# A decoder layer on one core: the order of the attention turns and of the start

## The chip, the cores and the metric

The kernel runs on one core of a Trainium2 chip. The metric is the device time of one execution in microseconds; lower is better. A core has five engines that run side by side, each in its own order: TensorE (PE, matrix products and transposes into PSUM banks), VectorE (DVE), ScalarE (ACT), GpSimd (POOL) and SyncE (SP, which here only issues DMAs). They wait for each other by semaphores.

## What is computed

One pre-norm decoder layer on x (32 sequences of 128 tokens, width 512), a context of 32 x 128 x 256 and two positions for each token:

```python
x = x + attn(layernorm(x))               # 16 heads of 32, rotary, causal
x = x + cross_attn(layernorm(x), ctx, pos)  # 32 heads of 16, axial rotary, + bout
x = x + ffn(layernorm(x))                # silu(gate) * up, 1408 wide, int weights with scales
```

Self-attention has q, k, v and output products with 512 x 512 weights. Cross-attention takes q from x and k, v from the context (one weight Wkv, 256 x 1024). Each softmax runs over the 128 keys of a sequence.

## The kernel before, in words

All products of the attention part are made of three passes with split operands: high half by high half, high by low, low by high, summed in one PSUM bank (`project`, L446). So each weight and each transposed activation needs a high half, made by ScalarE (a copy to the rounded type), and a low half, made by VectorE or GpSimd (original less high half).

The attention part is a software pipeline over the 32 sequences. `schedule` (L300) calls, on every engine, the function `turn(sq, cq, nx, nz, oq)`. In one turn five sequences are in work: `nz` is loaded and normalised, `nx` gets its self-attention q, k, v products, `sq` its self-attention scores, softmax and output product, `cq` its cross-attention (two rounds of 16 heads, called 2a and 2b), `oq` its last products with v and the output product. Turns 0 to 3 are written out, 27 turns run in a loop (`TURNS`), and four more follow. What each engine does in a turn, and in which order, is fixed by the order of the lines in its `turn`.

PE's turn before (L519): scores 1 (a mask product and 32 small products); the spread reciprocals of `oq` transposed (bank TC), `attend2("2b")` of `oq` (L501, products of the transposed probabilities with v); Wq2 product; Wo2 product; the v half of Wkv; T(q2); `transpose_prob("1")`; reciprocals of `sq` transposed; scores 2a; `attend1`; Wq1 product of `nx`; the k half of Wkv of `sq` (k2, TC); Wo1 product; `transpose_prob("2a")`; T(q1); scores 2b; `attend2("2a")`; Wk1 and Wv1 products; T(k2); `transpose_prob("2b")`; T(k1); T(z1), T(z2). Here T(k1) is the transpose of the rotated keys, and `collect` (L488) makes PE wait for the copies of transposed probabilities out of PSUM.

A rotated q or k is made in three steps: `rope` on VectorE (L778), two operations of 128 x 512 out of PSUM, then `rope_sum` on GpSimd (L380), one addition of two SBUF tiles, then the transpose on PE. q1 and q2 share one scratch buffer, k1 and k2 another. `spread` (L384) on GpSimd widens the reciprocals of the row sums to the head width; PE transposes them into TC, ScalarE copies them to rT1 or rT2 (L682, L669), and VectorE multiplies (`normalise_ctx`, L822). `normalise` (L766) is VectorE's layer norm: three operations on one element a partition, then z (L775), 128 x 512 from SBUF to SBUF. In a loop turn VectorE also reduces a window of the feed-forward weights (L915).

ScalarE's turn before (L661): rT2, the exponentials of scores 1 (L652, four banks of four), v2 and q2 copies, odd copies, rT1, exponentials and odd copies of 2a, q1 copy, exponentials 2b, v1 copy, odd copies 2b, high halves of z1T and z2T. VectorE copies the transposed k1 (L930).

At the start SyncE loads x of sequence 0, positions, then seven weights of 1 MB each. VectorE first makes the rotary angles (L730 to L754), then the norm of sequence 0, then the low halves of the first three weights; ScalarE makes the sines, the high halves of all seven weights in order, and loads the table for the exponentials (L709).

The lines around the last scores in PE's turn:

```python
                if has_c:
                    collect("2a", cq)
                    scores2("2b")
                    ...
                    attend2("2a")
                if has_n:
                    ...  # Wk1 and Wv1 products
                if has_s:
                    pe.wait_ge(rot["k2"], sq + 1)
                    transpose4(TC, columns(RA["k2"])).then_inc(rT_d["k2"], 1)
                if has_c:
                    transpose_prob("2b", cq)
                if has_n:
                    pe.wait_ge(rot["k1"], nx + 1)
                    transpose4(PA, columns(RA["k1"])).then_inc(rT_d["k1"], 1)
```

## Time and profile before

| | us |
|---|---|
| median of 3 runs | 1823.09 (1822.44 to 1823.45) |
| the profiled execution | 1822.44 |
| its span, first to last instruction | 1820.7 |
| PE matmul busy | 1693.9 (93%) |
| PE weight loads busy | 1376.9 (76%) |
| VectorE busy | 1158.4 (64%) |
| ScalarE busy | 964.3 (53%) |
| GpSimd busy | 480.6 (26%) |
| DMA, mean | 44 GB/s |

PE carries the work; the other engines set at which moments it has to wait. A share over the whole span says little here, as the start, the loop, the last turns and the feed-forward part (from about 1306 us) have different limits. In the rows of a timeline the first number is the start in us from the span's start, the second the time from the first start to the last end of the merged instructions, then engine, line, operation, what is written and read, shapes, and in brackets the idle time of the engine before it with what ended it.

### The profile page before, as it was taken

Reading aid. Unit: us, or ns where it says so; the run is one execution under the profiler, and the core shown is the slowest. Engines: PE = TensorE matmul, PEld = TensorE weight load, DVE = VectorE, ACT = ScalarE, POOL = GpSimd, SP = SyncE. Lnnn points to the kernel's source line nnn. Section 1 sums busy time; section 2 is a strip of 40 time slices with the busy share of each in tenths; the row PEclk is TensorE's granted clock in tenths of the full one; section 3 lists DMA queues with packets and bytes.
Section 4 is the critical chain, followed back from the end, with each engine's and each line's share of the span. In section 5 each row is a group of like instructions: output and inputs, shape, how many; then the busy total and the mean of one; then the engine's idle time right before and its main releaser. Section 6 shows DMA issues by size and latency. Waiting matters only on the chain. (4 is left out here: it accounts for less than half of the span.)

```text
span 1820.7 us, 36475 instructions
## 1 busy us (share of the span) xinstructions
PE 1693.9 (93%) x12704; PEld 1376.9 (76%) x12736; DVE 1158.4 (64%) x2143; ACT 964.3 (53%) x3791; POOL 480.6 (26%) x470
## 2 busy tenths in 40 slices
PE   4799999999999999999999999997899999999997
PEld 2577777777777777777777777776688888888885
DVE  4677777777777777777777777765564343444432
ACT  4366666666666666666666666665542222222221
POOL 1233333333334333343333333333001110110111
PEclk8899999999999999999999999998799999999999
DMA  5010110000101001010010100101332101110110
GB/s 194 15 32 19 32 46 28 33 28 28 50 28 33 28 28 50 28 33 28 28 50 28 33 28 28 36 29 58 107 107 70 69 0 69 69 59 10 69 46 24
DMA packets 55094, 80.93 MB, mean 44 GB/s; under 512 B 4880, under 2 KB 25488, under 8 KB 55056
## 3 DMA queue, kind: packets, MB, share of 16 engines
q1 hardware_dynamic: 55056, 80.43, 13.6%
q8 instruction: 24, 0.39, 0.1%
q14 instruction: 14, 0.11, 0.0%
HBM read 63.63 MB, written 16.78 MB: 44 GB/s over the span
## 5 line engine op out<-in xcount | busy, mean ns | idle before, releaser
L652 ACT ACTIVATE prob<-bank,nmax 128x128 f32<-128x128 f32 x1536 | 537.3, 405 | 108.3 <-DVE nmax L833 108.3
L652 ACT ACTIVATION_READ_ACCUMULATOR prob<-bank,nmax 128x1 f32 x1536 | 377.5, 246 | 0.0
L833 DVE TENSOR_REDUCE nmax<-bank 128x4 f32<-128x512 f32 x384 | 241.2, 684 | 97.0 <-PE bank L478 70.9
L1109 PE MATMUL fbank<-shared,piece_hi 128*128 128x512 f32 x1152 | 280.3, 394 | 0.0
L1109 PEld LDWEIGHTS fbank<-shared,piece_hi 128*128 128x128 f32 x1152 | 215.8, 187 | 53.2
L382 POOL TENSOR_TENSOR rope_buf<-rope_buf 128x512 f32<-128x512 f32 x128 | 165.2, 1291 | 300.3 <-DVE rope_buf L790 300.0
L456 PE MATMUL bank<-shared,z1T_h 128*128 128x512 f32 x768 | 204.3, 409 | 5.1 <-DVE shared L947 3.8
L443 PE MATMUL bank<-ident,prob 128*128 128x128 f32 x1536 | 191.9, 278 | 10.9 <-ACT prob L652 10.9
L1261 DVE SCALAR_TENSOR_TENSOR h<-fbank,su_c,sil 128x512 f32<-128x512 f32 x88 | 66.0, 750 | 206.1 <-PE fbank L1109 199.0
L443 PEld LDWEIGHTS bank<-ident,prob 128*128 128x128 f32 x1536 | 174.8, 143 | 20.5 <-ACT prob L652 16.5
L659 ACT ACTIVATE probT<-bank 128x512 f32<-128x512 f32 x192 | 115.3, 600 | 130.9 <-PE bank L443 130.8
L456 PEld LDWEIGHTS bank<-shared,z1T_h 128*128 128x128 f32 x768 | 142.0, 191 | 47.3 <-issue 16.4
L1195 ACT ACTIVATE sil<-fbank,sg_c 128x512 f32<-128x512 f32 x88 | 60.4, 687 | 174.6 <-PE fbank L1109 172.2
L1201 ACT ACTIVATE h_h<-h 128x512 fp32r<-128x512 f32 x88 | 55.6, 632 | 175.8 <-DVE h L1261 175.8
L839 DVE COPY probT<-bank 128x512 f32<-128x512 f32 x192 | 126.5, 685 | 17.0 <-PE bank L443 13.0
L401 POOL TENSOR_TENSOR cn_l<-cn,cn_h 128x512 fp32r<-128x512 f32 x64 | 82.7, 1292 | 186.0 <-DVE cn L825 186.0
L388 POOL TENSOR_TENSOR rbc<-rinv,one_c 128x512 f32<-128x512 f32 x64 | 66.5, 1038 | 234.7 <-DVE rinv L939 183.3
L1092 POOL TENSOR_TENSOR xr<-xr,ys 128x512 f32<-128x512 f32 x32 | 40.2, 1292 | 288.0 <-DVE ys L1281 288.0
L1124 PE MATMUL fbank<-piece_hi,h_h 128*128 128x512 f32 x288 | 115.3, 400 | 0.6 <-DVE h_l L1264 0.5
L1124 PE MATMUL fbank<-piece_hi,h_l 128*128 128x512 f32 x288 | 113.6, 395 | 0.0
L456 PE MATMUL bank<-shared,z1T_l 128*128 128x512 f32 x384 | 106.3, 399 | 0.0
L1264 DVE TENSOR_TENSOR h_l<-h,h_h 128x512 fp32r<-128x512 f32 x88 | 62.8, 714 | 61.4 <-ACT h_h L1201 61.4
(156 smaller groups left out, 2921.3 us busy)
## 6 DMA issues: line engine op xcount, KB each, us to landing
xA<-in_x SPq DMA_DIRECT2D x32, 256.0 KB, 2.9
xB<-in_x SPq DMA_DIRECT2D x32, 256.0 KB, 2.8
x_scratch<-x SPq DMA_DIRECT2D x32, 256.0 KB, 2.0
shared_loaded<-x_scratch SPq DMA_DIRECT2D x8, 1024.0 KB, 7.7
xr<-x_scratch SPq DMA_DIRECT2D x8, 1024.0 KB, 5.6
out<-xr SPq DMA_DIRECT2D x8, 1024.0 KB, 4.3
cx<-in_ctx SPq DMA_DIRECT2D x32, 128.0 KB, 2.2
range_window<-in_wg SPq DMA_DIRECT2D x27, 112.0 KB, 2.0
```

The costliest lines, as they stand in the source:

```text
L382: pool.tensor_tensor(RA[n][:, :], RA[n][:, :], RB[n][:, :], ALU.add).then_inc(rot[n], 1)
L388: pool.tensor_tensor(tile[:, :, :], r[:, :].unsqueeze(2).to_broadcast([P, h, w]), one_c[:, :].unsqueeze(2).to_broadcast([P, h, w]), ALU.mu ...
L401: pool.tensor_tensor(cn_l[:, :, :], cn[:, :, :], cn_h[:, :, :], ALU.subtract).then_inc(cn_lo[n], 1)
L443: last = nc.tensor.transpose(dst[:, j * P:(j + 1) * P], src(j), ident[:, :])
L456: last = nc.tensor.matmul(dst[:, :], a[:, j, :], w[:, j, cols], start=(n == 0), stop=(n == 3 * k - 1))
L652: last = nc.scalar.activation(prob[:, c, i, :], S[c][:, i * P:(i + 1) * P], ACT.Exp, bias=nmax[:, c, i:i + 1], accum_out=rs[:, h:h + 1])
L659: nc.scalar.activation(probT[:, c, :, :].rearrange("p g t -> p (g t)"), S[c][:, :], ACT.Copy).then_inc(pTo_r[kind(u)], 1)
L833: nc.vector.tensor_reduce(out=nmax[:, c, :], in_=S[c][:, :].rearrange("p (g k) -> p g k", g=G), op=ALU.max, axis=AX, negate=True).then_inc ...
L839: nc.vector.tensor_copy(probT[:, c, :, :].rearrange("p g t -> p (g t)"), S[c][:, :]).then_inc(pTe_r[kind(u)], 1)
L1109: last = nc.tensor.matmul(dst[:, :], w[:, k, cols], z[:, k, :], start=(n == 0), stop=(n == len(passes) * KT - 1))
L1124: last = nc.tensor.matmul(DN[s][:, :], a[j % 2][:, tok], w[piece][:, j % 2, :], start=(j == 0 and n == 0), stop=(j == HT - 1 and n == len( ...
L1261: nc.vector.scalar_tensor_tensor(out=h[j % 2][:, :], in0=UP[j % 2][:, :], scalar=su_c[:, j:j + 1], in1=sil[j % 2][:, :], op0=ALU.mult, op1 ...
```

## The change

Loop turns, PE: `attend2("2b")` goes in front of the transposed reciprocals of `oq`; the k half of Wkv goes from in front of Wo1 to behind T(q1), in front of the last scores; T(k1) goes in front of `transpose_prob("2b")`. ScalarE: the first bank of exponentials goes in front of rT2, and the copy of the transposed k1 comes from VectorE, behind the v1 copy. VectorE: rope k2 goes from behind rope q1 to behind the maxima of 2b, in front of `normalise(2)`. GpSimd: the rough reciprocal root goes in front of the k2 sum.

Start: positions are loaded behind Wq1, Wkv in front of Wo1. VectorE makes the norm of sequence 0 first, then angles, low halves and the table. The first products may begin with the high half of the weights. Turn 0 has its own function on PE (`first_projections`, k1 in bank TC), rope q1 and k1 stand at the head of VectorE's turn 0, z1T of sequence 1 is made in turn 1; turn 1 makes q1 of sequence 1 and k2 of sequence 0 (in bank PB) behind its first scores, and high halves of Wq2 and Wo2 are made in turn 1.

```diff
@@ PE
+            def first_projections():
+                pe.wait_ge(zT_hi[1], 1)
+                project(PA, z1T_h, z1T_l, "q1", KT, lo_ready=(zT_lo[1], 1), fresh=True).then_inc(pj["q1"], 1)
+                project(TC, z1T_h, z1T_l, "k1", KT, fresh=True).then_inc(pj["k1"], 1)
+                pe.wait_ge(zT_lo[1], 1)
+                project(PC, z1T_h, z1T_l, "v1", KT, fresh=True).then_inc(pj["v1"], 1)
+                pe.wait_ge(rot["q1"], 1)
+                transpose4(PA, columns(RA["q1"])).then_inc(rT_d["q1"], 1)
+                pe.wait_ge(rot["k1"], 1)
+                transpose4(TC, columns(RA["k1"])).then_inc(rT_d["k1"], 1)
...
+                if is_first(sq):
+                    pe.wait_ge(v1_r, 1)
+                    transpose_z1(1)
+                    project_q1(nx)
+                    pe.wait_ge(cxT_lo, 1)
+                    project(PB, cxT_h, cxT_l, "kv2", CKT, slice(0, D), fresh=True).then_inc(pj["k2"], 1)
                 if has_o:
+                    attend2("2b")
                     pe.wait_ge(rb_r[2], oq + 1)
...
                     transpose4(TC, columns(rbc2[:, :, :].rearrange("p h d -> p (h d)"))).then_inc(ri_d[2], 1)
-                    attend2("2b")
...
-                if has_s:
-                    pe.wait_ge(cxT_lo, sq + 1)
-                    pe.wait_ge(riT_r[1], sq + 1)
-                    project(TC, cxT_h, cxT_l, "kv2", CKT, slice(0, D), fresh=is_first(sq)).then_inc(pj["k2"], 1)
+                if has_n and has_c:
+                    project_q1(nx)
+                if has_s:
                     pe.wait_ge(cn_r[1], sq + 1)
                     project(PC, cn_h, cn_l, "o1", KT, lo_ready=(cn_lo[1], sq + 1), fresh=is_first(sq)).then_inc(pj["o1"], 1)
...
+                if has_s and has_c:
+                    pe.wait_ge(cxT_lo, sq + 1)
+                    pe.wait_ge(riT_r[1], sq + 1)
+                    project(TC, cxT_h, cxT_l, "kv2", CKT, slice(0, D)).then_inc(pj["k2"], 1)
...
-                if has_c:
-                    transpose_prob("2b", cq)
                 if has_n:
                     pe.wait_ge(rot["k1"], nx + 1)
                     transpose4(PA, columns(RA["k1"])).then_inc(rT_d["k1"], 1)
+                if has_c:
+                    transpose_prob("2b", cq)
@@ ScalarE
+                if has_s:
+                    exponentials("1", sq, (0,))
                 if has_o:
                     act.wait_ge(ri_d[2], oq + 1)
                     nc.scalar.activation(rT2[:, :], TC[:, :], ACT.Copy).then_inc(riT_r[2], 1)
                 if has_s:
-                    exponentials("1", sq)
+                    exponentials("1", sq, (1, 2, 3))
...
+                if has_n:
+                    act.wait_ge(rT_d["k1"], nx + 1)
+                    nc.scalar.activation(flat(kT1), (TC if is_first(nx) else PA)[:, :], ACT.Copy).then_inc(rT_r["k1"], 1)
@@ VectorE
+                if is_first(nx):
+                    rope("q1", nx, PA, DK1, cos1, sin1, DK1 ** -0.5)
+                    split_low(EARLY[2:])
+                    rope("k1", nx, TC, DK1, cos1, sin1, 1.0)
                 if has_s:
                     row_maxima("1", sq, range(G))
+                if is_first(sq):
+                    z1T_low(1)
+                    split_low(["kv2"])
+                    rope("q1", nx, PA, DK1, cos1, sin1, DK1 ** -0.5)
+                    first_copies()
...
                 if is_first(sq):
-                    split_low(["o1", "kv2"])
+                    rope("k2", sq, PB, DK2, *axial(sq), 1.0)
+                    split_low(["o1"])
...
                 if has_s:
-                    rope("k2", sq, TC, DK2, *axial(sq), 1.0)
                     dve.wait_ge(pj["o1"], sq + 1)
...
                     row_maxima("2b", cq, range(G))
+                if has_s and has_c:
+                    rope("k2", sq, TC, DK2, *axial(sq), 1.0)
                 if has_s:
                     normalise(2, x1A, z2, sq)
-                if is_first(sq):
-                    split_low(["q2", "o2"])
...
+                if is_first(sq):
+                    split_low(["q2", "o2"])
...
-                if has_n:
-                    dve.wait_ge(rT_d["k1"], nx + 1)
-                    nc.vector.tensor_copy(flat(kT1), PA[:, :]).then_inc(rT_r["k1"], 1)
...
             dve.wait_ge(x_in, 16)
             statistics(1, xA, 0)
             normalise(1, xA, z1, 0)
+            rotary_angles()
+            split_low(EARLY[:1])
             z1T_low(0)
-            split_low(EARLY)
+            split_low(EARLY[1:2])
+            rotary_table()
@@ GpSimd
+                if is_first(nx):
+                    rope_sum("q1", nx)
+                    rope_sum("k1", nx)
+                if is_first(sq):
+                    split_ctx(sq)
+                    rope_sum("q1", nx)
+                    rope_sum("k2", sq)
...
                 if sq is not None:
-                    rope_sum("k2", sq)
                     rough_rstd(2, sq)
-
-                if nx is not None:
+                    if cq is not None:
+                        rope_sum("k2", sq)
+
+                if nx is not None and sq is not None:
                     rope_sum("k1", nx)
```

`rotary_angles` and `rotary_table` are the lines L730 to L754 of before, moved.

## Rows read from the trace of the kernel before

**Rows 1.** By stretch: start:end, length, busy us per engine (count), PE clock, DMA.

```profile
0.00:81.50 81.50, 42.65 (x214) 31.91 (x217) 44.66 (x78) 28.41 (x55) 15.40 (x27) 0.83 0.34 117
...
156.00:1185.00 1029.00, 976.94 (x8830) 803.06 (x8856) 766.44 (x1459) 673.66 (x2997) 361.95 (x351) 1.00 0.11 33
```

**Rows 2.** Timeline of PE, one loop turn and the head of the next.

```profile
617.38 1.20 PE L456 MATMUL bank<-w_q_hi,z2T_h 128*128 128x512 f32 x4
...
632.47 0.62 PE L456 MATMUL bank<-w_kv_hi,cxT_h 128*128 128x512 f32 x2
...
636.60 1.91 PE L443 MATMUL bank<-ident,prob 128*128 128x128 f32 x16
...
639.29 1.15 PE L478 MATMUL bank<-kT,qT 32*128 32x256 f32 x16 [0.34 <-ACT probT L659]
...
647.06 0.60 PE L443 MATMUL bank<-ident,rope_buf 128*128 128x128 f32 x4
...
649.68 1.04 PE L443 MATMUL bank<-ident,z 128*128 128x128 f32 x8
...
651.26 0.81 PE L463 MATMUL bank<-causal,ident_b 128*128 128x512 bf16 x3 [0.55 <-DVE kT L930]
...
653.92 0.63 PE L443 MATMUL bank<-ident,rbc 128*128 128x128 f32 x4 [0.75 <-POOL rbc L388]
```

**Rows 3.** Timeline of VectorE, the same turn behind the last scores.

```profile
640.49 2.48 DVE L833 TENSOR_REDUCE nmax<-bank 128x4 f32<-128x512 f32 x4 [0.51 <-PE bank L478]
...
642.89 0.21 DVE L770 SCALAR_TENSOR_TENSOR nt<-r,ve 128x1 f32<-128x1 f32 x1
...
643.52 0.55 DVE L775 TENSOR_SCALAR z<-x1A,mv,nt 128x512 f32<-128x512 f32 x1
...
644.74 0.68 DVE L787 SCALAR_TENSOR_TENSOR rope_buf<-bank,cst 128x512 f32<-128x512 f32 x1
```

**Rows 4.** Timeline of GpSimd, the same stretch.

```profile
646.10 1.28 POOL L382 TENSOR_TENSOR rope_buf<-rope_buf 128x512 f32<-128x512 f32 x1 [5.50 <-DVE rope_buf L790]
...
652.64 1.04 POOL L388 TENSOR_TENSOR rbc<-rinv,one_c 128x512 f32<-128x512 f32 x1 [5.25 <-DVE rinv L939]
```

**Rows 5.** Feed-forward: VectorE beside GpSimd, and line L1264 (ns min/median/max).

```profile
1375.03 0.97 DVE L1264 TENSOR_TENSOR h_l<-h,h_h 128x512 fp32r<-128x512 f32 x1 [0.70 <-ACT h_h L1201]
...
1370.41 5.04 POOL L1092 TENSOR_TENSOR xr<-xr,ys 128x512 f32<-128x512 f32 x4 [30.12 <-DVE ys L1281]
...
L1264 DVE TENSOR_TENSOR h_l<-h,h_h x88: 691/693/972, 1311.7 to 1807.2; 128x512 fp32r<-128x512 f32 x88
```

**Rows 6.** Timeline of PE behind pauses, and one row by stretch.

```profile
78.42 1.12 PE L443 MATMUL bank<-ident,rope_buf 128*128 128x128 f32 x4 [3.41 <-POOL rope_buf L382]
...
90.45 0.66 PE L443 MATMUL bank<-ident,rope_buf 128*128 128x128 f32 x4 [1.33 <-POOL rope_buf L382]
...
1273.55 1.11 PE L443 MATMUL bank<-ident,prob 128*128 128x128 f32 x4 [2.41 <-ACT prob L652]
...
1298.11 1.21 PE L456 MATMUL bank<-w_o_hi,cn_h 128*128 128x512 f32 x4 [1.77 <-DVE cn L825]
...
1300.58 1.91 PE L456 MATMUL bank<-w_o_hi,cn_l 128*128 128x512 f32 x4
...
77.50:84.40 6.90, 5.76 (x43) 4.54 (x48) 2.92 (x5) 1.19 (x2) 0.87 (x1) 0.51 0.01 2
```

**Rows 7.** The first turns: timelines of VectorE and PE.

```profile
14.83 6.69 DVE L947 TENSOR_TENSOR shared<-shared_loaded,shared 128x2048 fp32r<-128x2048 f32 x3
...
26.78 0.69 DVE L760 BATCH_NORM_STATS2 st<-xA 128x6 f32<-128x512 f32 x1 [5.26 <-DMA xA<-in_x]
...
32.51 1.12 PE L443 MATMUL bank<-ident,rope_buf 128*128 128x128 f32 x4 [9.79 <-POOL rope_buf L382]
...
44.30 0.81 PE L463 MATMUL bank<-causal,ident_b 128*128 128x512 bf16 x3 [0.22 <-issue]
...
81.46 1.49 PE L463 MATMUL bank<-causal,ident_b 128*128 128x512 bf16 x3 [0.22 <-issue]
```

More of the change, by code:

```diff
@@ L642, in z1T_high, with exponentials @@
                 nc.scalar.activation(flat(z1T_h), PC[:, :], ACT.Copy).then_inc(zT_hi[1], 1)
-            def exponentials(u, q):
+            def exponentials(u, q, banks=range(G)):
                 rs = (rsum1, rsum2)[kind(u) - 1]
-                if u != "2b":
+                if u != "2b" and 0 in banks:
                     wait(act, ri_r[kind(u)], q)
-                for c in range(G):
+                for c in banks:
                     act.wait_ge(nmax_r[kind(u)], G * nth(u, q) + c + 1)
@@ L843, in z1T_low, with row_sums, first_copies @@
                 low(z1T_l, PC[:, :], z1T_h, zT_lo[1])
+            def row_sums(q):
+                dve.wait_ge(p_r[1], G * (q + 1))
+                wait(dve, rb_r[1], q)
+                nc.vector.reciprocal(rinv1[:, :], rsum1[:, :]).then_inc(ri_r[1], 1)
+            def first_copies():
+                row_sums(0)
+                even_copies("1", 0)
             def axial(q):
@@ L876, in turn @@
                     normalise(1, xA, z1, nz)
-                if has_s:
-                    dve.wait_ge(p_r[1], G * (sq + 1))
-                    wait(dve, rb_r[1], sq)
-                    nc.vector.reciprocal(rinv1[:, :], rsum1[:, :]).then_inc(ri_r[1], 1)
+                if has_s and has_c:
+                    row_sums(sq)
                     even_copies("1", sq)
@@ L918, in turn @@
                     ffn_normalise()
-                if has_n:
+                if has_n and has_s:
                     rope("k1", nx, PA, DK1, cos1, sin1, 1.0)
+                if is_first(sq):
+                    split_low(["q2", "o2"])
                 if has_s:
@@ L927, in turn @@
                     even_copies("2b", cq)
[L928 to L931 removed]
+                if nz is not None and has_s:
                     z1T_low(nz)
@@ L950, in _, with rotary_angles, rotary_table @@
             LOOP_STEPS = 8
+            def rotary_angles():
+                pos_t = pos_sb[:, :].rearrange("p (b c) -> p b c", c=2)
+                full_s = ang_s[:, :].rearrange("p (b c i) -> p b c i", b=B, c=2)
+                turns = turns_sb[:, :]
+                dve.wait_ge(pos_in, 16)
+                for i in range(HALF):
+                    last = nc.vector.tensor_scalar(full_s[:, :, :, i], pos_t, float(np.float32(10000.0 ** (-i / HALF))), None, ALU.mult)
+                link(last)
+                link(nc.vector.tensor_scalar(turns, ang_s[:, :], 1.0 / TWO_PI, MAGIC, ALU.mult, ALU.add))
+                link(nc.vector.tensor_scalar(turns, turns, MAGIC, None, ALU.subtract))
+                for part in (PI_A, PI_B, PI_C):
+                    link(nc.vector.scalar_tensor_tensor(out=ang_s[:, :], in0=turns, scalar=-part, in1=ang_s[:, :],
+                                                        op0=ALU.mult, op1=ALU.add))
+                link(nc.vector.tensor_scalar(ang_s[:, :], ang_s[:, :], math.pi - 1e-6, -(math.pi - 1e-6), ALU.min, ALU.max))
+                link(nc.vector.scalar_tensor_tensor(out=ang_c[:, :], in0=ang_s[:, :], scalar=-1.0, in1=ang_s[:, :],
+                                                    op0=ALU.mult, op1=ALU.max))
+                nc.vector.tensor_scalar(ang_c[:, :], ang_c[:, :], -1.0, math.pi / 2, ALU.mult, ALU.add).then_inc(tab, 1)
+            def rotary_table():
+                dve.wait_ge(tab_act, 2)
+                flat_s = ang_s[:, :].rearrange("p (b j) -> p b j", b=B)
+                flat_c = ang_c[:, :].rearrange("p (b j) -> p b j", b=B)
+                c2 = cos2[:, :, :].rearrange("p b (j e) -> p b j e", e=2)
+                s2 = sin2[:, :, :].rearrange("p b (j e) -> p b j e", e=2)
+                nc.vector.tensor_copy(c2[:, :, :, 0], flat_c)
+                nc.vector.tensor_copy(c2[:, :, :, 1], flat_c)
+                nc.vector.tensor_scalar(s2[:, :, :, 0], flat_s, -1.0, None, ALU.mult)
+                link(nc.vector.tensor_copy(s2[:, :, :, 1], flat_s))
             dve.wait_ge(x_in, 16)
```

90 lines of the change are left out of this document (41 added, 49 removed).

## The prediction

> **What bounds the kernel now.** The table by stretch comes first [rows 1]. 27 equal turns of the attention loop lie between 156 and 1185 us (TURNS is 27): 1029.0 us, 38.11 us a turn, TensorE (PE) busy 95% at a granted clock of 1.00. The first 81.5 us are another regime: PE busy half of the time, clock 0.83. From 1306 us on the feed-forward part runs, which the change doesn't touch. So there are two questions: what the first turns gain once, and what one loop turn gains or loses, times 27. In the second, a tenth of a microsecond is 2.7 us of the kernel.
>
> The second view is the timeline of PE in one loop turn [rows 2]. With U = 639.29 (start of the last scores, 2b), Z = 649.68 (z1 and z2 transposed), and Q = 617.38 (product with Wq2), a turn is Q to U 21.91, U to Z 10.39, Z to the next Q 5.81: 38.11. PE has only short pauses: 0.34 before U (behind ScalarE's copy of the last probabilities), 0.55 before the scores (behind VectorE's copy of the keys), 0.75 before the reciprocals are transposed (behind GpSimd). The third view is the timeline of VectorE and GpSimd behind U [rows 3, 4], because the change puts work there.
>
> **Part 1, what the loop turn gains.** (a) Products of the context keys (k2) stand in front of the last scores, no longer ahead of o1. Before, q1 ends at 632.47 and U is at 639.29, 6.82 later. Work between them is k2 1.40 + o1 2.73 (632.47 to 636.60 together), 1.75 of probabilities, 0.44 of queries: 6.32. The odd copy that U waited for is now hidden by k2's 1.40. Changing from products to scores costs 0.05 to 0.2, so the gain is 0.3 to 0.45; I take 0.4. The other input, cn and its low part, is early enough by about 1.7 us. (b) At the turn's end the key copy leaves VectorE, and attend 2b goes ahead of the transposed reciprocals. Z to the reciprocals is gated by z2's high copy, its low part, the reciprocal, and GpSimd's spread (652.64 in the next turn, 1.04 long), and PE starts them at Z + 4.24 in the next turn as in this one (653.92 against 649.68). That chain doesn't have the key copy in it and stays. But PE now has attend (1.0) done by then: scores at about Z + 1.2 instead of 1.58, over at Z + 3.1, attend to Z + 4.1, reciprocals at Z + 4.25, Q at Z + 4.75 instead of 5.81. Gain 1.05. (c) ScalarE does the first bank's exponentials ahead of rT2; the second context low part comes about 0.15 ahead of PE's need. Cost 0, at worst 0.3 if it slips. Sum of the gains 1.45 a turn.
>
> **Part 2, what the loop turn loses.** T(k1) moves in front of the 2b probabilities, and rope k2 moves on VectorE from behind rope q1 to behind the 2b maxima, in front of normalise 2, the window reduction and rope k1. PE reaches T(k1) at U + 8.21 (T(k2) at 647.06 is U + 7.77, plus 0.44). When is k1 ready? Steps from rows 3 and 4: maxima start U + 1.20 and take 2.40; rope k2 1.21 (two operations, as rope k1's pair: 644.74 to GpSimd's 646.10 less 0.08 of signal and the tail); normalise 2 and the window 1.85 (642.89 to 644.74); rope k1 1.28; signal 0.08; GpSimd's sum 1.29; signal to PE 0.24. Together U + 9.55. Before, without rope k2 and with 1.75 of probabilities in front of T(k1), nothing waited. PE now pauses 1.34, and 16 transposes that could have filled it are queued behind the waiting one; ScalarE's odd copies and VectorE's even copies wait for those.
>
> A second cost is in the same place. As soon as rope k2 is done, GpSimd begins its sum (U + 4.96 to about U + 6.3), and VectorE meets normalise 2: two tiny operations with two SBUF inputs, and z2 at U + 5.4. No row of the loop has normalise beside a GpSimd addition. The nearest rows are the feed-forward ones [rows 5]: h_l, two SBUF inputs, takes 0.69 alone, and 0.97 when it starts (1375.03) inside a GpSimd addition that ends at 1375.45; it ends 0.55 after that. It stood still until GpSimd was done. I take it that normalise 2 does the same: z2 waits for U + 6.3, 0.9 late, rope k1 starts at U + 7.6 and T(k1) at U + 10.5. The pause is 2.3 to 2.4. From below the cost is 0 (nothing is blocked), from above 1.2 (every small operation waits too); I take 0.95, by the h_l row.
> The Trainium skill says the same ("SBUF — State Buffer", SBUF: two separate sides): the port pair that VectorE and GpSimd share is a lock, held for a whole instruction, taken by VectorE in a two-port mode or with two SBUF inputs; the loser blocks fully. The h_l row agrees, and by the rule the cost comes out at the same 0.95.
>
> Net without the clock: -1.45 + 1.34 + 0.95 = +0.85 to +0.9 a turn, 27 x 0.9 = +24 us.
>
> **Part 3, the clock.** A pause of 2.3 us is of another kind than today's [rows 6]. Where PE was at full level (2.4 GHz) and paused 1.33 us (90.45), the clock held. Where it paused 1.77 us (1298.11) four matmuls took 1.21, and the third group of four 1.91: it fell to 1.2 GHz. Behind 3.41 (78.42) it fell too and stayed for 6.9 us at 0.51, and behind 2.41 (1273.55) four transposes took 1.11 instead of 0.60: three of three from 1.77 up. For the share of the turns in which it falls I choose 0.7, between never and always and nearer to always by these rows. At the low level for 6.9 us an engine that has work loses 3.4; a fall of half that length costs 1.7, and I take 2.0, as PE has work on both sides of the pause. 27 x 0.7 x 2.0 = +38 us. Bounds: 0 and 27 x 3.4 = 92; over 60 every stretch would have to be long.
>
> **Part 4, the first turns, once** [rows 7]. Before, q1's transposes start at 32.51 after an idle 9.79, because rope q1 stands on VectorE behind statistics that wait for x (26.78). Scores of batch 0 start at 44.30, of batch 1 at 81.46. After, the chain is VectorE's: z1 about 6.6 (its load is the first; normalising takes 3.1), angles 3.7 once pos has landed (8.5), the low half of Wq1 2.2 (three took 6.69) to 14.4, z1's low half, the low half of Wk1 to 17.3, table 1.0, rope q1 to 19.7, the low half of Wv1 to 21.9. PE: q1, k1, v1 from 14.6 to about 26, the transposes to 27, scores at 28: 16 us earlier. Turn 1 then takes 36 to 37 us as before (37.2): q1 and k2 products are earlier, but GpSimd waits for rope k2 ahead of its spread of the reciprocals, which puts these at scores + 17 where they were at + 13, and the low halves of Wq2 and Wo2 (2.2 each) again stand before kT2 on VectorE. Scores of batch 1 at about 64. Gain 17, between 12 and 20. Turns 2 and 3 have no window reduction, so their pause is 0.8 shorter: about 0.
>
> **Part 5, the last turns, once.** Attend goes into the 3 us for which PE waited for the last but one reciprocals (-1.8), T(k2) now waits for rope k2 in the last turn with scores (+0.5 to +1.5), and the last norm comes 0.7 later. About 0, within 1.5.
>
> **Sum.** The profiled execution took 1822.44 (span 1820.7, 1.7 around it); the median is 1823.09, 0.65 above. 1822.4 - 17 + 24 + 38 - 1 = 1866.
>
> **Rivals.** (B) The collision, but the clock holds: 1822.4 - 17 + 24 = 1830. For it: the pause has dense work on both sides, unlike the rows of falls, which lie among thin work. (C) The other side, no slower: normalise 2 isn't held. Its pieces before z2 are one element wide, and z2 itself has one SBUF input; only its 0.55 us, against the 0.68 of other operations of that width, speaks of two ports. (The Trainium skill, "VectorE: DVE Perf Modes", the perf-mode tier table, has tensor_scalar on fp32 in SBUF at the doubled rate; the 0.55 agrees.) Then the pause is 1.34, about the length at which the clock held, the turn is -1.45 + 1.34 = -0.1, and the kernel takes 1822.4 - 17 - 3 = 1802. It decides from a delay of normalise 2 under 0.5 us: then 17 us of the first turns outweigh the loop (break-even is +0.63 a turn). (D) The reordered start doesn't gain: low halves on VectorE and sums on GpSimd exclude each other there too, 5 to 8 us of the 17 go, and forecast and rivals all move up by so much.
>
> **How the numbers follow.** Forecast with falling clock 0.45 (1838 to 1888, by 0 to 60 us for the clock's term cut at the likely middle and 12 to 20 for the start), B 0.15 (1822 to 1840), C 0.30 (1795 to 1812), the rest, D among them, 0.10. The range has to take in C: 1799 to 1886. 0.2% is 3.6 us, about what a measurement of this kernel can tell from no change. Faster by more: C and a little of B, 0.31; within: 0.06; slower: 0.63.
>
> **What would show it.** In the trace of after: a turn of 40.3 us or more (forecast), 39.0 (B), 38.0 (C); PE idle before T(k1), released by GpSimd's rope_buf, 2.3 or 1.3 us; normalise 2's operations or z2 stretched to 1 us or more beside GpSimd's sum; granted clock of the loop about 0.95 instead of 1.00; the pauses before the last scores, the mask and the reciprocals gone; scores of batch 1 at 64 us. It is wrong if VectorE's normalise 2 shows its old 0.55 us beside the sum, if the clock stays at 1.00 through pauses of 2.3 us, or if PE meets another wait that I gave no cost, as ScalarE's later rT2 in front of o2.

## The result and the profile after

The changed kernel takes 1829.09 us (median of 6 runs, 1828.3 to 1831.66) against 1821.74 of the kernel before beside it (6 runs, 1820.43 to 1823.45): ratio 1.004, 95% interval 1.0028 to 1.0052. So it is slower, by 0.4%, where 2.4% was forecast; 1866 is missed by 37 us. The mechanism of rival B (the collision is there, the clock holds) is what happened; that its 1830 is met so closely is in part luck, as the part on why the prediction was wrong shows. The profiled execution took 1828.48 with a span of 1826.6, 5.9 longer than before.

Table by stretch of the changed kernel: the start up to the scores of the second sequence, the 27 loop turns, and the feed-forward part (columns as in [rows 1]: busy time and count of PE, its weight loads, VectorE, ScalarE and GpSimd, then PE's clock and the DMA).

```profile
0.00:68.00 68.00, 40.80 (x214) 30.77 (x217) 45.85 (x76) 29.13 (x58) 21.21 (x27) 0.87 0.40 140
143.10:1191.90 1048.80, 982.65 (x8829) 795.26 (x8856) 776.32 (x1431) 687.04 (x3024) 361.39 (x351) 1.00 0.11 32
1310.00:1826.60 516.60, 504.23 (x2224) 407.59 (x2224) 220.66 (x370) 144.31 (x220) 47.40 (x39) 0.99 0.17 62
```

The loop again runs at a granted clock of 1.00, but a turn takes 1048.8 / 27 = 38.85 us instead of 38.11 [rows 1]: +19.7 in all (from mask to mask the 27 turns took 1029.1 before). The loop begins 12.6 earlier (143.13 against 155.77), and the feed-forward part 5.9 later (1310.09 against 1304.20), so the last turns give back 1.2: -12.6 + 19.7 - 1.2 = +5.9.

TensorE in one loop turn of the changed kernel: the last scores, T(k2), T(k1), probabilities, T(z), the mask, the reciprocals, Wq2, Wo2 and the v half of Wkv behind it, Wo1 and the probabilities behind it, and the last scores of the next turn.

```profile
595.57 1.15 PE L491 MATMUL bank<-kT,qT 32*128 32x256 f32 x16
...
603.36 0.60 PE L454 MATMUL bank<-ident,rope_buf 128*128 128x128 f32 x4
...
605.78 0.66 PE L454 MATMUL bank<-ident,rope_buf 128*128 128x128 f32 x4 [1.82 <-POOL rope_buf L384]
...
606.27 1.91 PE L454 MATMUL bank<-ident,prob 128*128 128x128 f32 x16
...
608.02 1.04 PE L454 MATMUL bank<-ident,z 128*128 128x128 f32 x8
...
609.38 0.81 PE L476 MATMUL bank<-causal,ident_b 128*128 128x512 bf16 x3 [0.32 <-issue]
...
612.31 0.63 PE L454 MATMUL bank<-ident,rbc 128*128 128x128 f32 x4
...
612.70 1.18 PE L469 MATMUL bank<-w_q_hi,z2T_h 128*128 128x512 f32 x4
...
615.59 1.17 PE L469 MATMUL bank<-w_o_hi,cn_h 128*128 128x512 f32 x4
...
618.47 0.63 PE L469 MATMUL bank<-w_kv_hi,cxT_h 128*128 128x512 f32 x2
...
627.94 1.09 PE L469 MATMUL bank<-w_o_hi,cn_h 128*128 128x512 f32 x4
...
630.74 1.91 PE L454 MATMUL bank<-ident,prob 128*128 128x128 f32 x16
...
634.42 1.15 PE L491 MATMUL bank<-kT,qT 32*128 32x256 f32 x16
```

With U, Z and Q as in [rows 2]: U to Z is 12.45 (10.39 before), Z to Q 4.68 (5.81), Q to the next U 21.72 (21.91). The one long wait is that for GpSimd's sum of k1, 1.82. It stands in each of the 27 turns, at 1.82 to 1.84, and in each the four transposes behind it take 0.65 or 0.66: the clock doesn't fall. That is one execution; of the six that were timed (1828.3 to 1831.66) only this one has a trace.

The timeline of VectorE and GpSimd in the same stretch, in order of time (answers to [rows 3, 4]). VectorE has the maxima, rope k2, three one-element steps of the norm, z2, the window and rope k1; GpSimd has the sums of k2 (600.54) and of k1 (604.46).

```profile
596.79 2.48 DVE L858 TENSOR_REDUCE nmax<-bank 128x4 f32<-128x512 f32 x4 [1.51 <-PE bank L491]
...
599.19 0.68 DVE L812 SCALAR_TENSOR_TENSOR rope_buf<-bank,cos 128x512 f32<-128x512 f32 x1
...
600.38 0.21 DVE L791 SCALAR_TENSOR_TENSOR nt<-r,ve 128x1 f32<-128x1 f32 x1
...
600.54 1.29 POOL L384 TENSOR_TENSOR rope_buf<-rope_buf 128x512 f32<-128x512 f32 x1 [4.64 <-DVE rope_buf L815]
...
600.62 0.15 DVE L793 TENSOR_SCALAR nt<-nt 128x1 f32<-128x1 f32 x1
...
600.81 1.03 DVE L794 TENSOR_TENSOR nt<-nt,r 128x1 f32<-128x1 f32 x1
...
601.88 0.55 DVE L796 TENSOR_SCALAR z<-x1A,mv,nt 128x512 f32<-128x512 f32 x1
...
602.35 0.84 DVE L956 TENSOR_REDUCE range_per_window<-range_window 128x672 int32 x1
...
603.11 0.68 DVE L812 SCALAR_TENSOR_TENSOR rope_buf<-bank,cst 128x512 f32<-128x512 f32 x1
...
604.46 1.26 POOL L384 TENSOR_TENSOR rope_buf<-rope_buf 128x512 f32<-128x512 f32 x1 [2.63 <-DVE rope_buf L815]
```

The third step of the norm, a product of two columns of one element a partition (line L794), takes 1.03 us. In a place without an addition beside it, it takes 0.16 (shown under e1). It starts inside GpSimd's sum of k2 and ends with it: 600.81 + 1.03 = 601.84, and 600.54 + 1.29 = 601.83. z2 behind it has its old 0.55.

### The profile page after: what moved, and what is told of

Same layout as the page of the kernel before. It is cut to its first block and busy times, and to the rows that moved or that the text cites. A ratio compares the mean times of both kernels' runs of the same rounds, so it can differ in the third digit from the quotient of the medians.

```text
span 1826.6 us, 36448 instructions
## 1 busy us (share of the span) xinstructions
PE 1693.7 (93%) x12704; PEld 1365.3 (75%) x12736; DVE 1171.2 (64%) x2111; ACT 980.5 (54%) x3824; POOL 485.8 (27%) x470
## 5 line engine op out<-in xcount | busy, mean ns | idle before, releaser
L384 POOL TENSOR_TENSOR rope_buf<-rope_buf 128x512 f32<-128x512 f32 x128 | 170.1, 1329 | 315.2 <-DVE rope_buf L815 315.1
L454 PE MATMUL bank<-ident,prob 128*128 128x128 f32 x1536 | 187.9, 275 | 6.3 <-ACT prob L687 6.3
L454 PE MATMUL bank<-ident,rope_buf 128*128 128x128 f32 x512 | 79.0, 277 | 59.6 <-POOL rope_buf L384 59.6
L454 PEld LDWEIGHTS bank<-ident,rope_buf 128*128 128x128 f32 x512 | 60.4, 141 | 76.9 <-POOL rope_buf L384 67.8
```

The source lines that it names most:

```text
L384: pool.tensor_tensor(RA[n][:, :], RA[n][:, :], RB[n][:, :], ALU.add).then_inc(rot[n], 1)
L454: last = nc.tensor.transpose(dst[:, j * P:(j + 1) * P], src(j), ident[:, :])
```

## The experiments

All ratios are to the kernel before on the same chip; its median was 1820.47 for e1 to e4, 1821.09 for e5 to e8, 1820.12 for e9 to e12 and 1820.91 for e13 and e14. Turns are measured from one mask (or reciprocal) of the timeline to the next.

### e1: is it the place of rope k2?

```diff
+                if has_s and has_c:
+                    rope("k2", sq, TC, DK2, *axial(sq), 1.0)
                 if has_c:
                     row_maxima("2b", cq, range(G))
-                if has_s and has_c:
-                    rope("k2", sq, TC, DK2, *axial(sq), 1.0)
```

> The changed kernel, with rope k2 on VectorE in front of the 2b maxima instead of behind them; nothing else. Theory: the loop turn loses its 1.82 us pause ahead of T(k1) to two things in one place, 1.2 us of rope k2 on the chain maxima, normalise 2, window, rope k1, and 0.87 us for which normalise 2 stands still beside GpSimd's k2 sum. VectorE is idle 1.51 us ahead of the 2b maxima, and k2 is ready then. So both go: the maxima start at most 0.2 us later, the sum runs beside operations out of PSUM, T(k1) waits under 0.2 us, a turn takes 36.9 to 37.1 us instead of 38.85, the kernel 1775 to 1783. Rival: only the chain counts and the collision is an accident of the record: a turn of 37.6, the kernel 1795. Second rival: the later maxima delay the exponentials and with them the transposes of 2b by as much as the pause was: a turn of 38.5 or more.

Measured: 1775.43 (4 runs), ratio 0.9751 [0.9735, 0.9767], a turn of 37.01. The timeline behind the last scores, in order of time: VectorE's maxima, GpSimd's sum of k2, VectorE's third step of the norm and z2, then PE's T(k2) and T(k1) as one group without a wait:

```profile
609.53 2.48 DVE L858 TENSOR_REDUCE nmax<-bank 128x4 f32<-128x512 f32 x4
...
609.70 1.28 POOL L384 TENSOR_TENSOR rope_buf<-rope_buf 128x512 f32<-128x512 f32 x1 [1.26 <-DVE rope_buf L815]
...
612.36 0.16 DVE L794 TENSOR_TENSOR nt<-nt,r 128x1 f32<-128x1 f32 x1
...
612.55 0.55 DVE L796 TENSOR_SCALAR z<-x1A,mv,nt 128x512 f32<-128x512 f32 x1
...
615.89 1.24 PE L454 MATMUL bank<-ident,rope_buf 128*128 128x128 f32 x8
```

The sum of k2 now lies beside the maxima, which read one PSUM operand and aren't held (2.48, as before); the third step takes its 0.16, and the wait for k1 is gone. One moved call is worth 1.84 us a turn, and the rest of the change is then faster than the kernel before by 2.5%. The theory held. The edit takes away two things together, the 1.2 of rope k2 on the chain and the hold of 0.87; no run takes away the one without the other.

### e2: what exactly is held?

```diff
-                link(nc.vector.tensor_tensor(t[:, 3:4], t[:, 2:3], r0[n][:, :], ALU.mult))
+                link(nc.vector.tensor_scalar(t[:, 3:4], t[:, 2:3], r0[n][:, :], None, ALU.mult))
```

> The changed kernel, with the third small operation of normalise (t[2] times r0, two SBUF tensor inputs) written with r0 as a per-partition scalar, so that it has one tensor input. Theory 1, the pair of ports is needed by any fast SBUF operation: that operation goes through in 0.15 us, and z2 behind it, one input but doubled rate, is held until GpSimd's k2 sum ends; z2 takes 1.2 to 1.4 us instead of 0.55, the turn stays within 0.1 us of 38.85, the kernel within 1825 to 1830. Theory 2, only operations with two SBUF inputs are held: z2 keeps 0.55 us, the pause ahead of T(k1) falls from 1.82 to 1.0, a turn takes 38.0, the kernel 1805 to 1808.

Measured: 1821.1 (10 runs), ratio 0.9999 [0.9989, 1.0008], a turn of 38.55. In order of time, the sum of k2, the third step, z2, and T(k1):

```profile
595.60 1.30 POOL L384 TENSOR_TENSOR rope_buf<-rope_buf 128x512 f32<-128x512 f32 x1 [4.64 <-DVE rope_buf L815]
...
595.87 0.21 DVE L794 TENSOR_SCALAR nt<-nt,r 128x1 f32<-128x1 f32 x1
...
596.12 1.06 DVE L796 TENSOR_SCALAR z<-x1A,mv,nt 128x512 f32<-128x512 f32 x1
...
600.54 0.66 PE L454 MATMUL bank<-ident,rope_buf 128*128 128x128 f32 x4 [1.53 <-POOL rope_buf L384]
```

With one tensor input the step takes 0.21 and isn't held, but now z2 is: 1.06 instead of 0.55. So rival C of the prediction (z2 has one SBUF input, it isn't held) falls for its second reason as well. Both expected times are missed (1825 to 1830, and 1805 to 1808), and so is the expected length of z2 (1.2 to 1.4): the mechanism is the first theory's, but the turn is 0.30 shorter, because the held operation is now the last one of the norm. z2 ends 0.28 behind GpSimd's sum (595.60 + 1.30 = 596.90, 597.18), where after the held third step its whole 0.55 still followed. The Trainium skill ("SBUF — State Buffer", SBUF: two separate sides) has a lock on a shared port pair, for VectorE operations with two SBUF inputs or in a two-port mode, held for a whole instruction. This case's traces agree for both kinds: 1.03 for the two-input step, 1.06 for z2. For the one-element operations with one tensor input (0.15 and 0.21 beside the sum) they show no hold.

### e3 to e6: how long may the wait be?

Each adds to the loop turn one more reduction of the window in front of rope k1, whole or in part, so that only the wait for k1 grows:

```diff
+                    for i in range(1):
+                        nc.vector.tensor_reduce(out=rng_again[:, i:i + 1], in_=window[:, :, :].rearrange("p a n -> p (a n)"),
+                                                op=ALU.max, axis=AX, apply_absolute_value=True)
```

e4 has it twice; e5 and e6 once with `window[:, 0:1, :]` and `window[:, 0:2, :]`.

> The changed kernel, with the window reduction on VectorE made once more in each of the 27 loop turns (its result unused): 0.76 us more on the chain in front of rope k1, so the pause ahead of T(k1) goes from 1.82 to about 2.6 us. Theory a, the clock holds through pauses between dense work: 0.76 us a turn and no more, 20.5 us in all, 1848 to 1851, granted clock of the loop 1.00. Theory b, that of the prediction with a later threshold: somewhere above 1.82 us the clock falls; then the granted clock of the loop is under 0.98 and the kernel takes 1860 or more.

> The same with two more reductions: pause about 3.3 us in each of the 27 loop turns. Theory a: 41 us more than the changed kernel, 1869 to 1872, clock 1.00. Theory b: as behind the 3.41 us pause of the kernel before, the clock falls in most turns, 1.7 to 3.4 us each: 1890 to 1950, granted clock of the loop 0.90 to 0.95.

> The changed kernel with a third of the window reduced once more in each loop turn (result unused): about 0.3 us on the chain in front of rope k1, pause ahead of T(k1) about 2.1 us. The clock held at 1.82 (the changed kernel) and fell in most turns at 2.60 (one whole reduction more). If the limit lies above 2.1: 8 us more than the changed kernel, 1836 to 1839, clock of the loop 1.00. If below: 1855 or more, clock under 0.98.

> The same with two thirds of the window: about 0.53 us, pause about 2.35 us, which is the pause that the prediction reckoned with. If its clock term was right for its own pause, the loop's clock falls here in about seven turns of ten, some 2 us each: 1829 + 14 + 38 = 1881, at least 1865. If the clock holds: 1842 to 1845, and the term was wrong in itself, not only through the shorter pause.

| | wait for k1 | steady turn | clock, 200 to 1100 us | median | ratio |
|---|---|---|---|---|---|
| changed kernel | 1.82 | 38.85 | 1.00 | 1829.09 | 1.004 |
| e5 | 2.13 | 40.83 | 0.96 | 1873.22 | 1.0285 [1.0265, 1.0306] |
| e6 | 2.36 | 40.96 | 0.96 | 1881.43 | 1.033 [1.031, 1.0351] |
| e3 | 2.60 | 40.96 | 0.96 | 1884.78 | 1.0349 [1.0328, 1.037] |
| e4 | 3.35 | 41.7 to 43.0 | 0.95 | 1923.74 | 1.0563 [1.0542, 1.0584] |

The table's row of the loop from 200 to 1100 us and the timeline's row of T(k1) in one turn, of e5 and then of e6:

```profile
200.00:1100.00 900.00, 839.97 (x7233) 687.03 (x7254) 643.71 (x1196) 565.58 (x2485) 296.14 (x288) 0.96 0.10 31
```

```profile
217.48 1.12 PE L455 MATMUL bank<-ident,rope_buf 128*128 128x128 f32 x4 [2.13 <-POOL rope_buf L385]
```

```profile
200.00:1100.00 900.00, 834.25 (x7199) 681.46 (x7221) 645.30 (x1190) 562.01 (x2471) 295.79 (x287) 0.96 0.10 31
```

```profile
625.60 1.11 PE L455 MATMUL bank<-ident,rope_buf 128*128 128x128 f32 x4 [2.36 <-POOL rope_buf L385]
```

0.31 us more of waiting cost 44 us, of which 27 x 0.31 = 8.4 is the wait itself. In all four the clock falls, as theory b of e3 and e4 had it. The granted clock of the loop goes from 1.00 to 0.96, and the transposes behind the wait from 0.66 to as much as 1.12. In e5 23 of 26 turns take 40.55 to 40.84, and three take 39.15 to 39.18: those are the 38.85 + 0.31 of a turn whose clock held. So a turn with a fall costs 1.66 more. In e6 the one turn without a fall takes 39.40, and the others 1.4 to 1.6 more; in e3 it is 39.64 and 1.32. Between e6 and e3 the wait grows by 0.24 and the turn by nothing (40.96 in both), so the price of a fall isn't a constant. From never to nearly always falling it is the way from 1.82 to 2.13. In e5 the turns that hold come at equal distances (they begin at 142.76, 507.91 and 873.11, every ninth turn), with the same wait of 2.13 as the others: beside the length of the wait, the moment at which it comes counts.

e6's time was expected at 1881 by the prediction's clock term: 1881.43. Of its 52.3 above the changed kernel 0.54 x 27 = 14.6 is the longer wait itself and 37.7 the rest, where the prediction had 38 for the clock. The closeness is in part luck: in the trace e6's loop begins 1.7 earlier than the changed kernel's (141.38 against 143.13), and in that loop the clock costs 39.8 (1103.6 - 27 x 39.40). And 2.36 is the prediction's 2.3 to 2.4 only in number; in the profile's measure its chain is e5's 2.13, as the part on why the prediction was wrong shows. In e5 the clock costs 44.1 - 8.4 = 35.7.

### e7 and e10: attend in front of the reciprocals

e7 takes this part of the change back, e10 makes it alone in the kernel before (shown):

```diff
                 if has_o:
+                    attend2("2b")
                     pe.wait_ge(rb_r[2], oq + 1)
                     ...
                     transpose4(TC, ...).then_inc(ri_d[2], 1)
-                    attend2("2b")
```

> The changed kernel with one of its parts undone: attend 2b behind the transposed reciprocals again. Theory: GpSimd's spread gates the reciprocals at Z + 4.3 in either order, attend's 1.0 us then stands behind them, and PE pauses about 1.0 us in front: a loop turn takes 1.0 to 1.2 us more (39.9 to 40.0), the kernel 1857 to 1862. Rival: the order doesn't matter, since attend and reciprocals are both done by the time the product with Wq2 can start: under 3 us more.

> The kernel before with one edit: the last quarter of the prior sequence's products with V (attend 2b) stands ahead of the transposes of the reciprocals on TensorE. Theory 'cover': the wait for the spread reciprocals that stood ahead of the scores is filled; the prediction put this at 1.05 us in each of 28 turns, so 1792; e7, which undid it in the changed kernel, showed 1.3 a turn, so down to 1785. Range 1785 to 1797. Rival 'handed on': in the kernel before the next link (the query projection of the second attention, its rope, its row maxima) is late anyway, and less than 0.3 a turn is left: 1813 or more.

e7: 1865.39 (4 runs), 1.0246 [1.0229, 1.0263], a turn of 39.94 to 40.04, 1.14 more. e10: 1790.72 (4 runs), 0.9843 [0.9829, 0.9857], a turn of 37.17, 0.95 less. PE in e7 (reciprocals), then in e10 (reciprocals, Wq2):

```profile
625.58 0.63 PE L454 MATMUL bank<-ident,rbc 128*128 128x128 f32 x4 [0.97 <-POOL rbc L390]
```

```profile
640.35 0.66 PE L443 MATMUL bank<-ident,rbc 128*128 128x128 f32 x4
...
640.76 1.18 PE L456 MATMUL bank<-w_q_hi,z2T_h 128*128 128x512 f32 x4
```

In e7 PE waits 0.97 for the spread reciprocals; in e10, with attend in front, it doesn't wait. One moved call in the kernel before is worth 29 us; the prediction had 1.05 a turn for it. e7 is 3 to 8 us over its expected time, which counted the 27 loop turns alone. The rest lies in the last turns: from the loop's end to the feed-forward part they take 124.7 us (1222.24 to 1346.92) against 118.2 in the changed kernel (1191.93 to 1310.09), 6.5 more.

### e8, e9, e13: the start alone, and the places of the tiles

e8 has the changed start and the order of before in all full turns. e9 adds this, and e13 only its second half (the scratch tile from ahead of the activations to the end):

```diff
-        for n, _, k, m in WSRC[3:]:
+        for n, _, k, m in (WSRC[4], WSRC[3], WSRC[5], WSRC[6]):
...
-        tables = sb("table_scratch", [P, 2])
+        tables = sb("table_scratch", [P, 2])
```

> The changed start and first turns, with the order of the kernel before in all full turns (attend 2b behind the reciprocals, k2 in front of o1, rope k2 in front of x1A, T(k1) behind the probabilities, key copy on VectorE, exponentials in one piece). Theory: the start gives what the trace shows, scores of sequence 1 at about 68 us instead of 81.5, and nothing of it is lost later: 1806 to 1809, loop turn 38.11. Rival: part of the 13.5 us is given back in turns 2 and 3, or at the end: 1812 to 1818.

> The changed start with the order of the kernel before in all full turns, as in e8, and in addition every tile in SBUF at the place that it has in the kernel before: the weights are laid out with o1 ahead of kv2 (their transfers keep the new order), and the two-column scratch tile of the table loads, which stood ahead of the activations and shifted all of them by 8 bytes, stands last. In e8 the loop turn took 38.295 us against 38.115 before, and the groups of four matmuls of the output products stood 0.93 to 0.94 us apart against 0.90 to 0.91. Theory 'place': the addresses cost these 0.18 us; then the turn is 38.10 to 38.16 and the time 5 us under e8: 1808 to 1811. Rival 'order' (something of the start or of the program's length, whatever the addresses): the turn stays at 38.27 to 38.32 and the time at 1813 to 1816.

> e8 (changed start, order of before in full turns) with one half of e9: the two-column scratch tile stands last, so that the activations lie again at the distance from the weights that they had before; the weights keep the new order, kv2 ahead of o1. Theory 'shift': the 8 bytes did it, and the turn is 38.10 to 38.16 as in e9, the products with the low half of Wo 389 to 391 ns each. Rival 'weights': where the output weights lie did it, the turn stays at 38.28 to 38.31 and these products at 396. A turn between the two says that each has its part.

| | scores of the second sequence | turn | median | ratio |
|---|---|---|---|---|
| e8 | 69.21 | 38.30 | 1814.35 | 0.9958 [0.9941, 0.9974] |
| e9 | 66.74 | 38.11 | 1808.09 | 0.9941 [0.9928, 0.9954] |
| e13 | 68.22 | 38.11 | 1807.65 | 0.9924 [0.9909, 0.9939] |

e8 misses its expectation (1806 to 1809); it lies in the range of its rival (1812 to 1818), but not for the rival's reason, as the loop turn itself is longer. The products with the low half of the output weights from 200 to 1100 us (count, busy us, mean ns), from the groups by form, one block each for e8, e9 and e13:

```profile
L469 PE MATMUL bank<-w_o_lo,cn_h 128*128 128x512 f32 x188 | 51.5, 396 | 0.0
```

```profile
L469 PE MATMUL bank<-w_o_lo,cn_h 128*128 128x512 f32 x188 | 50.3, 389 | 0.0
```

```profile
L469 PE MATMUL bank<-w_o_lo,cn_h 128*128 128x512 f32 x188 | 50.2, 389 | 0.0
```

396 ns against 389: the 24 output products of a turn cost 24 x 0.007 = 0.17 us more in e8, which is its 0.18 a turn. The products with Wq2 keep their pace (395 to 396 in all three). e13 tells the cause: a tile of 8 bytes a partition in front of the activations shifts them against the weights, and with it moved the turn is 38.11 whichever order the weights have (e9, e13). Why the shift slows these products and not those with Wq2 stays open.

### e14: the changed kernel with its tiles at their old places

> The changed kernel, nothing else altered but the places of its tiles, as in e9. Theory 'place': its output products cost 396 ns as in e8 because of the addresses; with the old places 0.10 to 0.18 us of each turn come back, the turn is 38.67 to 38.75 against 38.85, and the time 2.7 to 7.5 us less, 1821 to 1826. What is then left of the turn's gain ahead of the last scores is 0.3 to 0.37 against 0.4 forecast. Rival: the pause ahead of the transposes of k1 grows by what the products save, as its length is set by VectorE and GpSimd counted from the last scores; then the saving must still show, since the products stand ahead of these scores: less than 0.05 a turn would count for the rival.

Measured: 1832.04 (5 runs), ratio 1.0063 [1.005, 1.0077]: not faster than the changed kernel, if anything slower. The wait for k1 in two turns:

```profile
217.26 0.66 PE L454 MATMUL bank<-ident,rope_buf 128*128 128x128 f32 x4 [1.85 <-POOL rope_buf L384]
...
256.03 1.03 PE L454 MATMUL bank<-ident,rope_buf 128*128 128x128 f32 x4 [1.85 <-POOL rope_buf L384]
```

The turn is 38.77, 0.08 shorter, and 27 x 0.08 = 2.2 us come back. But four of the 27 turns take 40.43: in them the clock falls, behind a wait of 1.85 instead of 1.82 to 1.84. 4 x 1.66 = 6.6 us are lost. Both expectations miss that. The four falls come every seventh turn (their transposes of k1 start at 256.03, 529.06, 802.09 and 1075.09), and the turns between have the same wait of 1.85. So here too the moment counts, and as the turn has another length, e14 doesn't tell whether the 0.01 to 0.03 us of wait did it or that its waits come at other moments. What it shows is that the changed kernel stands at the edge: with the same order of work and nearly the same wait its loop can lose the clock in some turns.

### e11 and e12: the second turn mended

e1's edit, and in the second turn GpSimd spreads the reciprocals ahead of the sum of k2, with the context's low half behind it. VectorE normalises the context ahead of o1's low half and makes o2's low half last (shown: GpSimd):

```diff
                 if is_first(sq):
                     split_ctx(sq)
                     rope_sum("q1", nx)
+                    spread(1, sq, rinv1, rbc1, H1, DK1)
                     rope_sum("k2", sq)
+                    ctx_low(1, sq)
```

> e1 (the rope of k2 ahead of the row maxima of 2b) and the second turn mended: on GpSimd the reciprocals of the first sequence are spread ahead of the rope sum of k2 and the context's low half stands right behind; on VectorE the context's normalisation stands ahead of o1's low half, and the low half of o2 at the end of the turn. In the changed kernel the transposes of the reciprocals in that turn waited 6.73 us for GpSimd, and the output product behind it ran at the low clock (5.1 us against 2.73). Theory 'path': 3 to 7 us of it are saved, 1768 to 1773. Rival 'weights': the output product waits for o1's low half, split later now, and the clock is low in this turn anyway: 1774 to 1779.

> e11 with the tiles at the places of the kernel before, as in e9. Theory 'place': 0.18 us in 27 turns, so 5 us under e11. Rival 'order': the same as e11 within 1.5 us.

e11: 1763.82 (5 runs), 0.969 [0.9678, 0.9703]. e12, with the places of e9: 0.9674 [0.9662, 0.9687], median 1761.91; five of its six executions lie at 1759.31 to 1763.05, one took 4253.64 and is unexplained. The timeline of the second turn, first of the changed kernel (o1's low half on VectorE and sum of k2 on GpSimd; reciprocals and output product on PE; q2's low half on VectorE, sum of k1 on GpSimd, o2's low half on VectorE; scores of the second sequence), then of e11 (reciprocals, output product with the high and with the low half, scores):

```profile
39.78 2.28 DVE L987 TENSOR_TENSOR w_o_lo<-w_o_lo_loaded,w_o_hi 128x2048 fp32r<-128x2048 f32 x1
...
39.94 3.24 POOL L384 TENSOR_TENSOR rope_buf<-rope_buf 128x512 f32<-128x512 f32 x1 [2.03 <-DVE rope_buf L815]
...
45.10 1.12 PE L454 MATMUL bank<-ident,rbc 128*128 128x128 f32 x4 [6.73 <-POOL rbc L390]
...
49.57 2.07 PE L469 MATMUL bank<-w_o_hi,cn_h 128*128 128x512 f32 x4 [1.48 <-DVE cn L850]
...
60.26 2.28 DVE L987 TENSOR_TENSOR w_q_lo<-w_q_lo_loaded,w_q_hi 128x2048 fp32r<-128x2048 f32 x1
...
60.42 3.24 POOL L384 TENSOR_TENSOR rope_buf<-rope_buf 128x512 f32<-128x512 f32 x1 [2.98 <-DVE rope_buf L815]
...
62.46 3.35 DVE L987 TENSOR_TENSOR w_o_lo<-w_o_lo_loaded,w_o_hi 128x2048 fp32r<-128x2048 f32 x1
...
67.95 1.37 PE L476 MATMUL bank<-causal,ident_b 128*128 128x512 bf16 x3
```

```profile
39.13 0.66 PE L455 MATMUL bank<-ident,rbc 128*128 128x128 f32 x4 [0.59 <-POOL rbc L390]
...
42.28 1.21 PE L470 MATMUL bank<-w_o_hi,cn_h 128*128 128x512 f32 x4 [1.48 <-DVE cn L851]
...
44.48 1.58 PE L470 MATMUL bank<-w_o_lo,cn_h 128*128 128x512 f32 x4 [0.99 <-DVE w_o_lo L993]
...
58.73 0.81 PE L477 MATMUL bank<-causal,ident_b 128*128 128x512 bf16 x3
```

In the changed kernel GpSimd's sum of k2 takes 3.24 instead of 1.29: VectorE's low half began 0.16 earlier, and the sum ends 1.12 behind the low half's end (43.18 against 42.06). So it is GpSimd that is held here. The reciprocals come behind the sum: PE waits 6.73 and goes on at the low clock (2.07 for four matmuls). The sum of k1 is held the same way at 60.42 by q2's low half, and o2's low half, which comes next on VectorE (62.46), takes 3.35 instead of 2.28 beside that sum (it ends at 63.66). With the spread in front the wait is 0.59, and the turn takes 34.3 us (24.46 to 58.73) against 41.1 in e1 and 43.4 in the changed kernel. e11 saves 11.6 us against e1 where 3 to 7 were expected. In the traces it is 9.7 at the start of the feed-forward part: 8.0 are there where the loop begins (138.71 to 130.75), 6.8 of them in this turn, and 1.4 come in the last turns; the remaining 2 are that e1's profiled execution (1773.06) was faster than its median. Four edits were made together, and no run tells them apart. The rival of the weights decides 0.99 us of wait at 44.48 and no more. e12's turn is 36.90 to e11's 37.00, and its median 1.9 lower, between its two expectations. Both are the fastest kernels of this study, 3.1 to 3.3% under the kernel before.

## Why the prediction was wrong, point by point

**Where it failed: the length of the wait, and from it the clock** (parts 2 and 3). The step that failed is the length of the wait and with it the clock term, 38 of the forecast's 44 us above the kernel before. It hung on one question: does a wait of this length, once a turn, lose the clock? The prediction answered "in 0.7 of the turns" for 2.3 to 2.4 us. The wait is 1.82, and it loses the clock in none of the 27 turns. Three things made the error.

- The chain was 0.29 too long: T(k1) came at U + 10.21, not 10.50. 0.18 of it is the signal from GpSimd to PE, taken as 0.24, which is what the reciprocals have in [rows 2, 4] (653.92 - (652.64 + 1.04)); the trace of the changed kernel has 605.78 - (604.46 + 1.26) = 0.06. The trace before had it too, at the wait of [rows 6] at 78.42: 78.42 - (77.10 + 1.26) = 0.06 (row below). 0.07 is the hold (0.88 against 0.95), the rest the sum of k1 (1.26 against 1.29) and roundings.
- Two measures of a wait were mixed. The prediction counted from PE's next possible start (T(k2) + 0.44), while the 1.33, 1.77 and 2.41 of [rows 6] count from the modelled end of the work before, which for T(k2) is T(k2) + 0.60. In the second measure the forecast's chain gives 2.13, the actual one 1.82. Those are e5 and the changed kernel: at 2.13 the clock falls in nearly every turn, at 1.82 in none. Had the wait been as long as forecast, the clock term would have been about right.
- The rows for the limit came from thin work. At 1.77 the clock fell in [rows 6] behind other pauses; in the loop it holds at 1.82 to 1.84, behind e5's 2.13 it falls again. The prediction named this as what speaks for rival B, and gave B 0.15. How much of the difference is the work around the wait, and how much the moment at which it comes, no run tells.

The sum of k1 on GpSimd in front of the wait at 78.42, in the trace of the kernel before:

```profile
77.10 1.26 POOL L382 TENSOR_TENSOR rope_buf<-rope_buf 128x512 f32<-128x512 f32 x1 [6.90 <-DVE rope_buf L790]
```

**The price of a fall was right by compensation.** 2.0 a turn was taken for 0.7 of the turns; e5 shows 1.66 in 23 of 26, e6 about 1.55 in all but one. The product, 1.4 a turn, is what e6's time gives (37.7 / 27).

**The hold** (part 2) was right: one small operation with two SBUF inputs stands still until GpSimd's addition ends, 0.88 us (1.97 + 0.76 from the norm's start to rope k1, 2.73, less the 1.85 before). It was the third step and not z2, which changes nothing here; in e2 it does.

**The gains of the turn** (part 1). (b) 1.05 forecast, 1.13 in the changed kernel, 0.95 alone in e10. (c) nothing, as forecast. (a) 0.4 forecast, 0.19 seen. The reordering itself gives its 0.41: from the end of q1's products to U it is now 6.48 (627.94 to 634.42), less 0.07 by which the o1 products in it have grown, against 6.82. But the output products take 0.22 more a turn (o2's from 2.73 to 2.88, 615.59 to 618.47; o1's from 2.73 to 2.80, 627.94 to 630.74); 0.08 of it is the 8-byte shift (e14), the other 0.14 stays open. From U to Z the turn loses 2.06 (12.45 against 10.39). It comes out at -0.19 + 2.06 - 1.13 = +0.74, 19.7 us in the 27 turns against 24. The prediction's own terms add up to +0.84, which it took as 0.9: 1.6 of the 24 us are that rounding.

**The start** (part 4). Scores of the first sequence at 24.59, even 3.4 before the forecast's 28; of the second at 67.95 instead of 64, -13.5 instead of -17, and 0.9 less at the loop. The reciprocals are at 45.10, forecast 45, but the turn takes 43.4 and not 36 to 37. What was left out is the low clock behind a wait of 6.73, which was foreseen as a wait and not as a clock, and the halves held beside the sums (rival D, in part). The changed start alone is worth 6.7 us with the shift (e8) and 12.0 without it (e9).

**The last turns** (part 5): about 0, within 1.5; they gave 1.2.

Put into the forecast's sum: 1822.4 - 12.6 + 19.7 + 0 - 1.2 = 1828.3, against the profiled execution's 1828.48. Rival B had the same terms at -17 and +24: its start was 4.4 too good and its loop 4.3 too dear, and that these two cancel is luck.

## What to carry to other kernels

Before moving an operation on VectorE, look at what GpSimd will do right behind it. An addition of SBUF tiles that begins there stopped the next VectorE operation with two SBUF inputs, even one of one element a partition (1.03 instead of 0.16), and the 128 x 512 step from SBUF to SBUF in e2 (1.06 instead of 0.55); put a reader of PSUM behind it (e1: one call, 1.84 us a turn). Cost a recurring wait of PE in two cases, clock kept and clock lost, and compare lengths in one measure. Where it comes out near a length at which the clock fell, shorten it until it is well clear, since here 0.31 us of wait decided over 44 us of the kernel.

## What the runs showed of the hardware that was not expected

- A product of two columns of one element a partition took 1.03 us instead of 0.16 beside an addition on GpSimd.
- The clock held at 1.00 through 27 waits of 1.82 to 1.84 between dense work, fell in 4 of 27 turns at 1.85 and in 23 of 26 at 2.13; a fall cost 1.3 to 1.7 us of the turn. At 1.85 the falls came every seventh turn, at 2.13 the turns without a fall every ninth.
- GpSimd can be the one that is held: its sum took 3.24 instead of 1.29 when a VectorE operation with two SBUF inputs (2.28) had begun 0.16 before it.
- A tile of 8 bytes a partition in front of the activations made the output products 396 ns instead of 389, 0.18 us a turn, with the same instructions.
